# Token recurrence of a transformer kernel: one decay matrix and two products computed on GpSimd instead of VectorE

## The chip, the core and the metric

The kernel runs on one core of one Trainium2 chip. Its metric is the device time of one execution in microseconds (us), the median of three runs. In the rows PE is TensorE (PEld its weight loads), DVE is VectorE, ACT is ScalarE, POOL is GpSimd and SP is SyncE. All the matrices of this stage are float32 and lie in the on-chip memory SBUF, 128 partitions wide.

## The reference, cut to the stage that is changed

The reference is a decoder of twelve stages over 32 sequences of 64 tokens with 256 channels. The second stage is a recurrence over the tokens of each sequence, channel by channel. `k` is the layer-normed input, `v` the context, `w` and `u` are one number per channel:

```
def step(carry, kv_t):
    p, q, o = carry
    kt, vt = kv_t
    no = jnp.maximum(o, u + kt)
    A = jnp.exp(o - no)
    E = jnp.exp(u + kt - no)
    y = (A * p + E * vt) / (A * q + E)
    no2 = jnp.maximum(w + o, kt)
    A2 = jnp.exp(w + o - no2)
    E2 = jnp.exp(kt - no2)
    return ((A2 * p + E2 * vt, A2 * q + E2, no2), y)
...
x = x + _L0_xattn_ref(32, 64, 256, L0_xattn_w, L0_xattn_u, _layernorm(x, axis=-1), ctx_2048)
```

`E` is what the title calls the own factor: the weight of the token's own value `vt`.

## The kernel before, in words

The stages run one after the other, each in a block of its own that all engines enter and leave together. The changed stage is `l0_xattn`. It keeps channels on the 128 partitions and all 2048 tokens (32 sequences of 64) along a partition, so the 256 channels make two blocks, c = 0 and c = 1, and nearly every instruction covers 128 x 2048 elements.

VectorE carries the stage, in program order: `maxima(0)`, `maxima(1)`, `sums(0)`, `sums(1)`, `quotient(0)`, `quotient(1)`, `added(0)`, `added(1)`.

- `maxima(c)` fills `ws` (in the rows `wkv_ws`), the decay matrix: `w` of the channel in every column, and a very negative number in the first column of each of the 32 sequences, so that one scan can run over all sequences. It takes a memset to zero (L748), an addition of `w` (L751), and a small memset (L753). The scan L755 reads it and gives the running maxima `om`. From these come the exponents `a2`, `e2`, `e1`, `no`.
- `sums(c)` waits for ScalarE's exponentials, and runs the scans for `q` (`qb`, L771) and `p` (`pb`, L773). L775 and L777 make the denominator; L778 makes the prior part of the numerator, L779 the product of own factor `e1` (kept in `core_XN`) and value `v` (`core_CT`), L781 their sum.
- `quotient(c)` waits for ScalarE's reciprocal, `added(c)` adds the transposed result to the residual `X`.

ScalarE copies the shifted maxima (L809), takes the exponentials (L813 to L819; the semaphore `exp1_ready` rises after L819) and the reciprocals (L824, L826). TensorE transposes the context at the start and the results at the end. GpSimd has no instruction in this stage. The order on each engine is the order of the code; engines wait for each other by semaphores, and `drain()` makes an engine finish what it has begun before it goes on.

Of the kernel before, what the change touches and what calls it, by code (L numbers as in the profile page):

```python
# [17 lines left out]
ALU = mybir.AluOpType  # L18
# [3 lines left out]
P = 128  # L22
B, S, D = 32, 64, 256
TOK = B * S
NT = TOK // P
BPT = P // S
DC = D // P
# [677 lines left out]
NEG_INIT = -1e38  # L705


def l0_xattn(nc, g, a):

    with ExitStack() as ctx:  # L710
        s = Scope(nc, g, ctx, "wkv")
        wu = s.sb("wu", [P, 2, DC])
        tv, qb = s.sb("tv", [P, TOK]), s.sb("qb", [P, TOK + 1])
        loaded = s.sem("loaded")
# [5 lines left out]
        def early(sp):  # L720
# [6 lines left out]
        om, op, no, a2, e2 = [[s.sb(f"{n}{c}", [P, TOK]) for c in range(DC)] for n in ("om", "op", "no", "a2", "e2")]  # L727
        e1 = [xn[:, c, :] for c in range(DC)]
        ws = s.sb("ws", [P, TOK])
        pb = s.sb("pb", [P, TOK + 1])  # L730
        pt = s.ps("pt", [P, DC, NCH, CH])
        (ct_ready, ct_done, max_ready, prev_ready, decay_ready, own_ready, prior_ready, exp_ready, exp1_ready, den_ready, rcp_ready, yT_ready,
         t_ready) = s.sem(
            "ct_ready", "ct_done", "max_ready", "prev_ready", "decay_ready", "own_ready", "prior_ready", "exp_ready", "exp1_ready", "den_ready",
            "rcp_ready", "yT_ready", "t_ready")
        by_batch = lambda t: t[:, 0:TOK].rearrange("p (b t) -> p b t", t=S)
        with nc.Block() as block:

            @block.vector
            def _(dve):  # L740
                dve.memset(pb[:, 0:1], 0.0)
                dve.memset(qb[:, 0:1], 0.0)
                dve.wait_ge(loaded, 16)

                def maxima(c):
                    k = g.XT[:, c, :]
                    w, u = wu[:, 0, c:c + 1], wu[:, 1, c:c + 1]
                    dve.memset(ws[:, :], 0.0)  # L748
                    dve.memset(by_batch(op[c])[:, :, 0:1], NEG_INIT)
                    dve.drain()  # L750
                    dve.tensor_scalar(ws[:, :], ws[:, :], w, None, ALU.add)  # L751
                    dve.drain()
                    dve.memset(by_batch(ws)[:, :, 0:1], NEG_INIT)  # L753
                    dve.drain()
                    dve.tensor_tensor_scan(om[c][:, :], ws[:, :], k, NEG_INIT, ALU.add, ALU.max).then_inc(max_ready, 1)  # L755
                    dve.drain()
                    dve.tensor_tensor(e2[c][:, :], k, om[c][:, :], ALU.subtract)
                    dve.wait_ge(prev_ready, c + 1)
                    dve.scalar_tensor_tensor(no[c][:, :], k, u, op[c][:, :], ALU.add, ALU.max)
                    dve.scalar_tensor_tensor(a2[c][:, :], op[c][:, :], w, om[c][:, :], ALU.add, ALU.subtract).then_inc(decay_ready, 1)  # L760
                    dve.drain()
                    dve.scalar_tensor_tensor(e1[c], k, u, no[c][:, :], ALU.add, ALU.subtract).then_inc(own_ready, 1)
                    dve.tensor_tensor(no[c][:, :], op[c][:, :], no[c][:, :], ALU.subtract).then_inc(prior_ready, 1)

                def sums(c):
                    v = g.CT[:, c, :]
                    dve.wait_ge(exp_ready, c + 1)
                    if c == 0:
                        dve.wait_ge(ct_done, 1)
                    dve.tensor_tensor(tv[:, :], e2[c][:, :], v, ALU.mult)  # L770
                    dve.tensor_tensor_scan(qb[:, 1:TOK + 1], a2[c][:, :], e2[c][:, :], 0.0, ALU.mult, ALU.add)  # L771
                    dve.drain()
                    dve.tensor_tensor_scan(pb[:, 1:TOK + 1], a2[c][:, :], tv[:, :], 0.0, ALU.mult, ALU.add)  # L773
                    dve.wait_ge(exp1_ready, c + 1)
                    dve.tensor_tensor(om[c][:, :], no[c][:, :], qb[:, 0:TOK], ALU.mult)  # L775
                    dve.drain()
                    dve.tensor_tensor(om[c][:, :], om[c][:, :], e1[c], ALU.add).then_inc(den_ready, 1)  # L777
                    dve.tensor_tensor(op[c][:, :], no[c][:, :], pb[:, 0:TOK], ALU.mult)  # L778
                    dve.tensor_tensor(tv[:, :], e1[c], v, ALU.mult)  # L779
                    dve.drain()  # L780
                    dve.tensor_tensor(op[c][:, :], op[c][:, :], tv[:, :], ALU.add)  # L781
                    dve.drain()

                def quotient(c):
                    dve.wait_ge(rcp_ready, c + 1)
                    dve.tensor_tensor(op[c][:, :], op[c][:, :], om[c][:, :], ALU.mult).then_inc(yT_ready, 1)

                def added(c):
                    for n in range(NCH):
                        dve.wait_ge(t_ready, c * NCH + n + 1)  # L790
                        xs = g.X[:, n * TPC:(n + 1) * TPC, c * P:(c + 1) * P]
                        dve.tensor_tensor(xs, xs, pt[:, c, n, :].rearrange("p (j d) -> p j d", d=P), ALU.add)

                maxima(0)
                maxima(1)
                sums(0)
                sums(1)
                quotient(0)
                quotient(1)
                added(0)  # L800
                added(1)

            @block.scalar
            def _(act):
                act.preload_act_table_set("natural_log_exp_and_others")

                def previous(c):
                    act.wait_ge(max_ready, c + 1)
                    act.activation(by_batch(op[c])[:, :, 1:S], by_batch(om[c])[:, :, 0:S - 1], ACT.Copy).then_inc(prev_ready, 1)  # L809

                def exponentials(c):
                    act.wait_ge(decay_ready, c + 1)
                    act.activation(a2[c][:, :], a2[c][:, :], ACT.Exp)  # L813
                    act.activation(e2[c][:, :], e2[c][:, :], ACT.Exp)
                    act.drain().then_inc(exp_ready, 1)
                    act.wait_ge(own_ready, c + 1)
                    act.activation(e1[c], e1[c], ACT.Exp)
                    act.wait_ge(prior_ready, c + 1)
                    act.activation(no[c][:, :], no[c][:, :], ACT.Exp)  # L819
                    act.drain().then_inc(exp1_ready, 1)  # L820

                def reciprocals(c):
                    act.wait_ge(den_ready, c + 1)
                    act.activation(om[c][:, :], om[c][:, :], ACT.Ln)  # L824
                    act.drain()
                    act.activation(om[c][:, :], om[c][:, :], ACT.Exp, scale=-1.0).then_inc(rcp_ready, 1)  # L826

                def context():
                    for k in range(NCH * DC):
                        i, c = k // DC, k % DC  # L830
                        act.wait_ge(ct_ready, k + 1)
                        last = act.activation(g.CT[:, c, i * CH:(i + 1) * CH], pt[:, c, i, :], ACT.Copy)
                    last.then_inc(ct_done, 1)

                previous(0)
                context()
                exponentials(0)
                previous(1)
                exponentials(1)
                reciprocals(0)  # L840
                reciprocals(1)

            @block.tensor
            def _(pe):
                for i in range(NCH):
                    pe.wait_ge(cx_loaded[i], 16)
                    for c in range(DC):
                        for j in range(TPC):
                            mm = pe.transpose(pt[:, c, i, j * P:(j + 1) * P], cx[i][:, j, c * P:(c + 1) * P], g.ident[:, :])
                        mm.then_inc(ct_ready, 1)  # L850
                for c in range(DC):
                    pe.wait_ge(yT_ready, c + 1)
                    for n in range(NCH):
                        for j in range(TPC):
                            t0 = n * CH + j * P
                            mm = pe.transpose(pt[:, c, n, j * P:(j + 1) * P], op[c][:, t0:t0 + P], g.ident[:, :])
                        mm.then_inc(t_ready, 1)
# [2123 lines left out]


LEVELS = [l0_attn, l0_xattn, l0_ffn, l1_attn, l1_xattn, l1_ffn, l2_attn, l2_xattn, l2_ffn, l3_attn, l3_xattn, l3_ffn]


# [175 lines left out]
```

## Time and profile before

| | before |
|---|---|
| time, median of 3 runs | 4816.47 us (4814.08 to 4819.29) |
| time of the profiled execution | 4816.8 us |
| span of the profiled execution | 4815.0 us, mean granted TensorE clock 0.936 |
| the changed stage and its surroundings, 202 to 296 us | 94.0 us, 2.0% of the span |
| VectorE busy in those 94 us | 91.70 us |
| ScalarE / TensorE / GpSimd busy in them | 31.25 / 9.50 / 0.00 us |

The span runs from the first to the last instruction; 1.8 us of the time lie outside it. A row of the timeline gives start, duration, engine, line, operation, tile written and tiles read, shape, count and, in brackets, how long the engine had been idle and what ended that.

### The profile page before, as it was taken

The page shows a single profiled execution, that of the slowest core. Times are in us where ns is not written, and L with a number is a line of the kernel's source. Part 1 is how long each engine was busy: PE and PEld are TensorE (multiplying, and loading weights), DVE is VectorE, ACT ScalarE, POOL GpSimd, SP SyncE. Part 2 cuts the span into 40 slices and gives each one's busy share as a digit, 9 for nine tenths or more (in the row PEclk, how much of TensorE's full clock was granted, in tenths as well). Part 3 has the DMA queues.
Part 4 walks back from the last instruction along what each step waited for, and adds up shares of the span by engine and source line. Part 5 has one row for each costly group of instructions (what it writes and reads, how often), then busy time and mean ns, then how long its engine had stood idle before and what let it go on. Part 6 is the DMA issues. An engine that isn't in the chain of part 4 may idle for free. (4 is left out here: it accounts for less than half of the span.)

```text
span 4815.0 us, 142985 instructions
## 1 busy us (share of the span) xinstructions
PE 4134.3 (86%) x62044; PEld 2706.1 (56%) x62052; DVE 3237.9 (67%) x6019; ACT 2128.8 (44%) x3774; POOL 1514.5 (31%) x1605
## 2 busy tenths in 40 slices
PE   8527886677777887997999999999999999779999
PEld 6415654323325664443677777777777777445555
DVE  7897734788897787744677777777777777531111
ACT  3545533654444554322555555555555555221111
POOL 1001200198893220000344433443334433212222
PEclk9868987889889998998999999999999999789999
DMA  1000000133341001001000000000001000031111
GB/s 34 19 27 11 2 12 20 59 119 122 118 141 42 2 2 33 20 0 40 12 24 21 21 21 24 22 21 21 21 22 26 21 17 4 8 125 54 50 53 44
DMA packets 72967, 175.11 MB, mean 36 GB/s; under 512 B 14578, under 2 KB 27892, under 8 KB 69748
## 3 DMA queue, kind: packets, MB, share of 16 engines
q1 hardware_dynamic: 72340, 165.96, 11.1%
q8 instruction: 490, 8.03, 0.7%
q14 instruction: 137, 1.12, 0.1%
HBM read 163.04 MB, written 2.88 MB: 34 GB/s over the span
## 5 line engine op out<-in xcount | busy, mean ns | idle before, releaser
L1684 POOL TENSOR_TENSOR ssm_ub<-ssm_dtu,ssm_bcn 128x512 f32<-128x512 f32 x256 | 324.5, 1294 | 305.0 <-DMA ssm_bcn<-ssm_bct 302.6
L2437 POOL TENSOR_TENSOR dn_eb<-dn_ee,dn_cc 128x512 f32<-128x512 f32 x64 | 66.7, 1042 | 1043.4 <-DVE dn_cc L2551 1043.4
L2977 DVE TENSOR_TENSOR moe_hh<-moe_si,moe_pu 128x512 f32<-128x512 f32 x104 | 71.4, 687 | 450.6 <-PE moe_pu L2866 444.3
L2481 DVE SCALAR_TENSOR_TENSOR core_XN<-dn_bA,dn_w,core_XN 128x504 f32<-128x504 f32 (+2 forms) x384 | 280.6, 731 | 44.0 <-ACT core_XN L2318 24.0
L1583 ACT ACTIVATE ssm_da<-core_XN,ssm_al 128x504 f32<-128x504 f32 x240 | 163.2, 683 | 254.0 <-DVE ssm_ph L1751 169.4
L2144 PE MATMUL dn_bA<-core_XT,dn_w 128*128 128x512 f32 x512 | 259.3, 630 | 18.7 <-DVE core_XN L2481 13.4
L2910 ACT ACTIVATE moe_si<-moe_pg 128x512 f32<-128x512 f32 x104 | 62.1, 597 | 467.1 <-PE moe_pg L2866 467.1
L2929 POOL TENSOR_TENSOR moe_hw<-moe_hh,moe_cb 128x512 f32<-128x512 f32 x100 | 126.4, 1264 | 451.3 <-DVE moe_hh L2977 393.2
L1570 PE MATMUL ssm_py<-ssm_hc,core_ident 128*128 128x512 f32 x352 | 201.0, 674 | 65.0 <-DVE ssm_hc L1755 34.9
L2276 PE MATMUL dn_po<-dn_wo,dn_cT 128*128 128x256 f32 x1024 | 242.3, 390 | 3.3 <-issue 2.2
L1751 DVE TENSOR_TENSOR_SCAN ssm_ph<-ssm_da,ssm_ub 128x512 f32<-128x512 f32 x168 | 205.0, 1220 | 30.0 <-POOL ssm_ub L1684 17.1
L2168 PEld LDWEIGHTS dn_pm<-dn_XB,dn_mb 32*32 32x32 f32 x16384 | 166.8, 105 | 92.2 <-issue 86.4
L2419 POOL TENSOR_TENSOR dn_gm<-dn_cb,dn_cs 128x256 f32<-128x256 f32 x128 | 76.7, 620 | 447.6 <-DMA dn_cb<-dn_cum 447.6
L309 POOL TENSOR_TENSOR a_ke<-a_qkT,a_kmask 128x512 f32<-128x512 f32 (+1 forms) x96 | 85.5, 911 | 410.4 <-DVEq L600 303.8
L2168 PEld LDWEIGHTS dn_pm<-dn_zz,dn_XB 32*32 32x32 f32 x16384 | 164.8, 105 | 88.4 <-issue 87.7
L2276 PEld LDWEIGHTS dn_po<-dn_wo,dn_cT 128*128 128x128 f32 x1024 | 192.0, 192 | 31.1 <-issue 2.7
L2168 PE MATMUL dn_pm<-dn_XB,dn_mb 32*32 32x32 f32 x16384 | 195.8, 195 | 4.6 <-DVE dn_XB L2492 3.1
L2866 PE MATMUL moe_pg<-core_XT,moe_w 128*128 128x512 f32 x416 | 198.1, 599 | 0.0
L2866 PE MATMUL moe_pu<-core_XT,moe_w 128*128 128x512 f32 x416 | 195.5, 592 | 0.0
L2168 PE MATMUL dn_pm<-dn_zz,dn_XB 32*32 32x32 f32 x16384 | 193.2, 194 | 0.5 <-ACT dn_zz L2327 0.5
L2881 PE MATMUL moe_py<-moe_w,moe_hw 128*128 128x256 f32 x800 | 188.7, 379 | 0.0
L2881 PEld LDWEIGHTS moe_py<-moe_w,moe_hw 128*128 128x128 f32 x800 | 152.0, 190 | 62.4 <-issue 46.9
(521 smaller groups left out, 10450.2 us busy)
## 6 DMA issues: line engine op xcount, KB each, us to landing
ssm_bcn<-ssm_bct SPq DMA_DIRECT2D x128, 512.0 KB, 3.7
dn_cb<-dn_cum SPq DMA_DIRECT2D x32, 512.0 KB, 4.8
dn_w<-in_dn_w SPq DMA_DIRECT2D x32, 388.0 KB, 3.3
moe_cb<-moe_rows SPq DMA_DIRECT2D x64, 192.0 KB, 2.8
moe_w<-in_moe_w SPq DMA_DIRECT2D x26, 384.0 KB, 9.8
moe_cb<-moe_rows SPq DMA_DIRECT2D x64, 128.0 KB, 3.0
dn_wo<-in_dn_w SPq DMA_DIRECT2D x16, 256.0 KB, 5.1
moe_cb<-moe_rows SPq DMA_DIRECT2D x64, 64.0 KB, 2.6
```

The source lines that it names most:

```text
L309: last = pool.tensor_tensor(dst[:, c, :, :], bcm(src[:, c, :], R), bc(kmask[:, :], P), ALU.mult)
L1570: pe.matmul(py[:, turn_ % 2, :], g.ident[:, :], src[:, :], start=n == 0, stop=n == N - 1).then_inc(add_done, 1)
L1583: act.activation(nb(factor(u))[:, :, 1:S], nb(dt[q % 2][:, c, :])[:, :, 1:S], ACT.Exp, scale=al[:, n, c:c + 1]).then_inc(da_ready, 1)
L1684: pool.tensor_tensor(ub[u % NUB][:, :], dtu[q % 2][:, c, :], bcn[i % NB][:, 0, :], ALU.mult).then_inc(ub_ready, 1)
L1751: dve.tensor_tensor_scan(ph[:, m % 2, :], factor(u), ub[u % NUB][:, :], 0.0, ALU.mult, ALU.add).then_inc(scan_done, 1)
L2144: mm = pe.matmul(bank[:, :], wp[:, kc, gi * P:(gi + 1) * P], g.XT[:, kc, q * CH:(q + 1) * CH], start=kc == 0, stop=kc == DC - 1)
L2168: mm = pe.matmul(bank[r, n * HB:(n + 1) * HB], left(n, r), right(n, r), start=True, stop=True, tile_position=(q * HB, q * HB))
L2276: mm = pe.matmul(po[:, j // 2, (j % 2) * D:(j % 2 + 1) * D], cT[:, 2 * j + h, :], wo[o // NCH % 2][:, h, :], start=h == 0, stop=h == 1)
L2481: last = dve.scalar_tensor_tensor(dst[:, :, n:S], src[:, :, 0:S - n], w[i // NCH % 2][:, at:at + 1], dst[:, :, n:S], ALU.mult, ALU.add)
L2866: mm = pe.matmul(dst[:, m % 2, :], w[:, k, at:at + P], g.XT[:, kc, n * CH:(n + 1) * CH], start=kc == 0, stop=kc == DC - 1)
L2881: mm = pe.matmul(py[:, j, 0:D], h[:, j * P:(j + 1) * P], w[:, k, DC * 2 * P:], start=k == 0, stop=k == G - 1)
L2929: pool.tensor_tensor(hw[m % 3][:, :], hh[m % 3][:, :], cb[j % NCB][:, :], ALU.mult).then_inc(hw_ready, 1)
```

## The change

GpSimd gets instructions in this stage. It builds the second block's decay matrix in a tile of its own, `ws1`; VectorE still builds the first block's, and for c = 1 waits on `wait_ready` before the scan. GpSimd also computes the product of own factor and value for both blocks, into `ov0` and `ov1`, as soon as `exp1_ready` tells that the exponentials of the block are there; VectorE waits on `own_v_ready` where it adds the product. Two semaphores and three tiles of 128 x 2048 are new.

```diff
         by_batch = lambda t: t[:, 0:TOK].rearrange("p (b t) -> p b t", t=S)
+        ws1 = s.sb("ws1", [P, TOK])
+        ov = [s.sb(f"ov{c}", [P, TOK]) for c in range(DC)]
         with nc.Block() as block:
+
+            @block.gpsimd
+            def _(pool):
+                pool.wait_ge(loaded, 16)
+                pool.memset(ws1[:, :], 0.0)
+                pool.drain()
+                pool.tensor_scalar(ws1[:, :], ws1[:, :], wu[:, 0, 1:2], None, ALU.add)
+                pool.drain()
+                pool.memset(by_batch(ws1)[:, :, 0:1], NEG_INIT).then_inc(wait_ready, 1)
+                pool.wait_ge(ct_done, 1)
+                for c in range(DC):
+                    pool.wait_ge(exp1_ready, c + 1)
+                    pool.tensor_tensor(ov[c][:, :], e1[c], g.CT[:, c, :], ALU.mult).then_inc(own_v_ready, 1)
...
                 def maxima(c):
                     k = g.XT[:, c, :]
                     w, u = wu[:, 0, c:c + 1], wu[:, 1, c:c + 1]
-                    dve.memset(ws[:, :], 0.0)
                     dve.memset(by_batch(op[c])[:, :, 0:1], NEG_INIT)
-                    dve.drain()
-                    dve.tensor_scalar(ws[:, :], ws[:, :], w, None, ALU.add)
-                    dve.drain()
-                    dve.memset(by_batch(ws)[:, :, 0:1], NEG_INIT)
-                    dve.drain()
-                    dve.tensor_tensor_scan(om[c][:, :], ws[:, :], k, NEG_INIT, ALU.add, ALU.max).then_inc(max_ready, 1)
+                    if c == 0:
+                        dve.memset(ws[:, :], 0.0)
+                        dve.drain()
+                        dve.tensor_scalar(ws[:, :], ws[:, :], w, None, ALU.add)
+                        dve.drain()
+                        dve.memset(by_batch(ws)[:, :, 0:1], NEG_INIT)
+                        dve.drain()
+                    else:
+                        dve.wait_ge(wait_ready, 1)
+                    dve.tensor_tensor_scan(om[c][:, :], (ws, ws1)[c][:, :], k, NEG_INIT, ALU.add, ALU.max).then_inc(max_ready, 1)
...
                     dve.tensor_tensor(op[c][:, :], no[c][:, :], pb[:, 0:TOK], ALU.mult)
-                    dve.tensor_tensor(tv[:, :], e1[c], v, ALU.mult)
                     dve.drain()
-                    dve.tensor_tensor(op[c][:, :], op[c][:, :], tv[:, :], ALU.add)
+                    dve.wait_ge(own_v_ready, c + 1)
+                    dve.tensor_tensor(op[c][:, :], op[c][:, :], ov[c][:, :], ALU.add)
```

On VectorE, in the second `maxima`, the row behind the last row of `maxima(0)` and up to the first of the exponents stood before as follows (the scans are printed as SCALAR_TENSOR_TENSOR).

```order
L763 TENSOR_TENSOR wkv_no<-wkv_op,wkv_no 128x2048
L748 MEMSET wkv_ws 128x2048
L749 MEMSET wkv_op 128x32
L751 TENSOR_SCALAR wkv_ws<-wkv_ws,wkv_wu 128x2048
L753 MEMSET wkv_ws 128x32
L755 SCALAR_TENSOR_TENSOR wkv_om<-wkv_ws,core_XT 128x2048
L757 TENSOR_TENSOR wkv_e<-core_XT,wkv_om 128x2048
```

And now, at the same place:

```order
L781 TENSOR_TENSOR wkv_no<-wkv_op,wkv_no 128x2048
L763 MEMSET wkv_op 128x32
L773 SCALAR_TENSOR_TENSOR wkv_om<-wkv_ws,core_XT 128x2048
L775 TENSOR_TENSOR wkv_e<-core_XT,wkv_om 128x2048
L777 SCALAR_TENSOR_TENSOR wkv_no<-core_XT,wkv_wu,wkv_op 128x2048
```

Three rows on the decay matrix are gone from there; in each `sums` the row of L779 is gone likewise. On GpSimd, between the stage of attention before it (a_xs, a_ke) and the next one, this now stands (before, nothing stood between the branch of L290 and that of L292).

```order
L290 UNCONDITIONAL_BRANCH
L741 UNCONDITIONAL_BRANCH
L744 MEMSET wkv_ws 128x2048
L746 ISA
L746 TENSOR_SCALAR wkv_ws<-wkv_ws,wkv_wu 128x2048
L748 MEMSET wkv_ws 128x32
L752 TENSOR_TENSOR wkv_ov<-core_XN,core_CT 128x2048 x2
L739 UNCONDITIONAL_BRANCH
L292 UNCONDITIONAL_BRANCH
```

The five operations have come to GpSimd; here `wkv_ws` stands for the new tile `ws1`, since the rows leave numbers out.

## Rows read from the trace of the kernel before

**Rows 1.** Page head.
```profile
span 4815.0 us, 142985 instructions
```

**Rows 2.** Windows, one stretch: length, PE, PEld, DVE, ACT, POOL busy; clock.
```profile
202.00:296.00 94.00, 9.50 (x64) 9.02 (x63) 91.70 (x46) 31.25 (x23) 0.00 (x0) 0.55 0.00 0
```

**Rows 3.** Waits from 201 to 310 us, row on the memsets: total, times, longest.
```profile
DVE wkv_ws L748 <- issue: 0.8, 2, 0.4
```

**Rows 4.** Timeline of VectorE in the stage.
```profile
204.28 1.28 DVE L751 TENSOR_SCALAR wkv_ws<-wkv_ws,wkv_wu 128x2048 f32<-128x2048 f32 x1
...
205.85 4.42 DVE L755 TENSOR_TENSOR_SCAN wkv_om<-wkv_ws,core_XT 128x2048 f32<-128x2048 f32 x1
...
219.55 2.28 DVE L763 TENSOR_TENSOR wkv_no<-wkv_op,wkv_no 128x2048 f32<-128x2048 f32 x1
222.21 1.76 DVE L748 MEMSET wkv_ws<- 128x2048 f32 x1 [0.38 <-issue]
...
225.69 4.42 DVE L755 TENSOR_TENSOR_SCAN wkv_om<-wkv_ws,core_XT 128x2048 f32<-128x2048 f32 x1
...
257.17 2.28 DVE L778 TENSOR_TENSOR wkv_op<-wkv_no,wkv_pb 128x2048 f32<-128x2048 f32 x1
...
259.37 2.28 DVE L779 TENSOR_TENSOR wkv_tv<-core_XN,core_CT 128x2048 f32<-128x2048 f32 x1
261.72 2.29 DVE L781 TENSOR_TENSOR wkv_op<-wkv_op,wkv_tv 128x2048 f32<-128x2048 f32 x1
...
286.60 4.49 DVE L786 TENSOR_TENSOR wkv_op<-wkv_op,wkv_om 128x2048 f32<-128x2048 f32 x2
```

**Rows 5.** Timeline of ScalarE in the stage.
```profile
222.85 1.89 ACT L819 ACTIVATE wkv_no<-wkv_no 128x2048 f32<-128x2048 f32 x1
...
242.68 1.89 ACT L819 ACTIVATE wkv_no<-wkv_no 128x2048 f32<-128x2048 f32 x1
...
281.78 1.91 ACT L826 ACTIVATE wkv_om<-wkv_om 128x2048 f32<-128x2048 f32 x1
```

**Rows 6.** Groups of GpSimd's instructions by shape: busy, mean ns, idle before.
```profile
L2434 POOL TENSOR_SCALAR dn_wo<-dn_wo,dn_nw 128x512 f32<-128x512 f32 x16 | 25.1, 1567 | 0.0
...
L2699 POOL TENSOR_TENSOR core_XN<-core_XN,lk_gb 128x1024 f32<-128x1024 f32 x4 | 9.4, 2348 | 42.2 <-ACT core_XN L2674 42.2
...
L296 POOL MEMSET a_ve<- 128x1024 f32 x3 | 2.8, 952 | 270.6 <-SPq L290 248.1 <-POOLq L111 22.5
```

**Rows 7.** L1751's instructions by source: min/median/max ns; `ssm_da` in PSUM, `ssm_dx` in SBUF.
```profile
L1751 DVE TENSOR_TENSOR_SCAN ssm_ph<-ssm_da,ssm_ub x168: 1203/1222/1232, 937.3 to 1470.2; 128x512 f32<-128x512 f32 x168
L1751 DVE TENSOR_TENSOR_SCAN ssm_ph<-ssm_dx,ssm_ub x8: 1204/1714/2223, 981.6 to 1395.8; 128x512 f32<-128x512 f32 x8
```

**Rows 8.** Timeline of VectorE and GpSimd around 981 us.
```profile
981.60 1.21 DVE L1751 TENSOR_TENSOR_SCAN ssm_ph<-ssm_dx,ssm_ub 128x512 f32<-128x512 f32 x1
981.76 2.10 POOL L1673 TENSOR_TENSOR ssm_hp<-ssm_hb,ssm_bcn 128x512 f32<-128x512 f32 x1 [3.24 <-DVE ssm_hb L1746]
```

**Rows 9.** The same from 4167 to 4175 us; all tiles in SBUF.
```profile
4167.04 1.40 DVE L2723 TENSOR_TENSOR_SCAN lk_st<-lk_kd,lk_xi 128x512 f32<-128x512 f32 x1 [1.71 <-ACT lk_xi L2662]
4167.31 3.28 POOL L2695 TENSOR_TENSOR core_X<-core_X,lk_gb 128x1024 f32<-128x1024 f32 x1
4169.55 2.13 DVE L2723 TENSOR_TENSOR_SCAN lk_st<-lk_kd,lk_xi 128x512 f32<-128x512 f32 x1 [0.33 <-ACT lk_xi L2662]
4170.55 3.26 POOL L2695 TENSOR_TENSOR core_X<-core_X,lk_gb 128x1024 f32<-128x1024 f32 x1
4172.52 1.57 DVE L2730 TENSOR_SCALAR lk_mr<-lk_ms 128x512 f32<-128x512 f32 x1
4174.02 0.41 DVE L2730 TENSOR_SCALAR lk_mr<-lk_ms 128x512 f32<-128x512 f32 x1
```

**Rows 10.** The same around 445 us; all tiles in SBUF.
```profile
445.22 2.14 DVE L628 TENSOR_TENSOR a_sc<-a_sc,a_mx 128x512 f32<-128x512 f32 x2
445.34 1.47 POOL L309 TENSOR_TENSOR a_ke<-a_qkT,a_kmask 128x512 f32<-128x512 f32 x1 [1.13 <-ACTq L498]
```

More of the change, by code:

```diff
@@ L732, in l0_xattn @@
         (ct_ready, ct_done, max_ready, prev_ready, decay_ready, own_ready, prior_ready, exp_ready, exp1_ready, den_ready, rcp_ready, yT_ready,
-         t_ready) = s.sem(
+         t_ready, wait_ready, own_v_ready) = s.sem(
             "ct_ready", "ct_done", "max_ready", "prev_ready", "decay_ready", "own_ready", "prior_ready", "exp_ready", "exp1_ready", "den_ready",
-            "rcp_ready", "yT_ready", "t_ready")
+            "rcp_ready", "yT_ready", "t_ready", "wait_ready", "own_v_ready")
         by_batch = lambda t: t[:, 0:TOK].rearrange("p (b t) -> p b t", t=S)
+        ws1 = s.sb("ws1", [P, TOK])
+        ov = [s.sb(f"ov{c}", [P, TOK]) for c in range(DC)]
         with nc.Block() as block:
+            @block.gpsimd
[10 more added lines that the diff above has]
+                    pool.tensor_tensor(ov[c][:, :], e1[c], g.CT[:, c, :], ALU.mult).then_inc(own_v_ready, 1)
             @block.vector
```

## The prediction

> **What bounds the kernel now.** I read the table of windows first. The changed stage is 94 us of a span of 4815 us, and VectorE is busy in 91.7 of them, with ScalarE at a third and GpSimd at nothing [rows 1, 2]. So VectorE alone sets the length of this stage. The table of waits confirms it: VectorE waits for no other engine there, and the only entry is 0.4 us of "issue" ahead of each of the two long memsets [rows 3]. The timeline of VectorE then gives the prices: the instructions stand back to back, a product of 128x2048 every 2.20 us where no drain lies between, and a scan takes 4.42 us [rows 4]. Whatever VectorE loses or gains here, the stage loses or gains, since the block ends with VectorE's additions, and the next stage cannot begin before. Last I looked for places elsewhere in the trace at which GpSimd and VectorE work on SBUF at the same time, because the stage has none of its own. They decide the case.
>
> **What VectorE is relieved of.** The second `maxima`: L763 ends at 219.55 + 2.28 = 221.83, and the scan L755 starts at 225.69 [rows 4]. In these 3.86 us stand the two memsets, the addition and three drains. One small memset (0.09) stays, so 3.8 us go. The gap of 0.38 us ahead of the long memset goes with it; it belongs to that memset. The products: L779 starts 2.20 us behind L778, and L781 follows as before, behind a drain [rows 4]. Removed in both `sums`: 4.4 us. Together VectorE has **8.2 us** less of its own work. Nothing takes its place as a dependence: the second `maxima` and the last steps wait for ScalarE as little as before. The tightest is the last reciprocal, ready at 281.78 + 1.91 = 283.69 [rows 5]. `quotient(1)`, the second of the pair from 286.60, started at about 288.8 [rows 4]; counted from the denominator that the reciprocal waits for, it now comes the 2.2 us of one product earlier, at 286.6, and 2.9 us remain.
>
> **Whether GpSimd is in time.** Its product for c = 0 can start when `exp1_ready` rises, at 222.85 + 1.89 = 224.74, and VectorE wants it behind L778, at 259.45; for c = 1 it is 244.57 [rows 4, 5] against about 282. The decay matrix is wanted at 221.8. GpSimd needs a few us for each, so the two new waits cost nothing, and neither does the later end of GpSimd in the block. The price lies elsewhere.
>
> **What GpSimd's instructions do to VectorE.** Of the scans L1751, the 168 that read their factor from PSUM took 1203 to 1232 ns; the 8 that read both inputs from SBUF took 1204 to 2223 ns [rows 7]. The timeline shows why. At 4167.04 a scan with both inputs in SBUF runs till 4168.44. GpSimd's L2695, begun at 4167.31, ends at 4170.59, 2.15 us behind the scan's end, although this shape takes 2.35 alone. The next scan begins at 4169.55 and ends at 4171.68, 1.09 behind GpSimd's end (alone 1.21 [rows 8]). GpSimd's next ends at 4173.81, 2.13 behind that scan, and L2730, an addition on VectorE that takes 0.41 alone, ends 0.28 behind that, after 1.57 [rows 6, 9]. They take turns: one runs, the other stands still. Around 981 us it is the same at 512 elements: GpSimd ends 1.05 behind the scan [rows 8]. And VectorE having the next instruction ready does not keep GpSimd out: the two L628 back to back took 2.14 us where two of that length take 1.3 (2.28 / 4 plus some start each), with GpSimd's instruction ending 0.55 us ahead of the pair's end [rows 4, 10]. All work of VectorE in this stage from L751 on has two SBUF inputs, or is the addition L751 that behaves as L2730. So each of GpSimd's three long instructions stops VectorE for about its own length, and VectorE has no idle time to take it from.
>
> Prices. The product: GpSimd ended 1.05 us behind the scan at 512 elements and 2.14 at 1024, so 1.09 per 512 more, and 2.14 + 2 x 1.09 = 4.3 at 2048 (alone 2.35 + 2 x 1.09 = 4.5). VectorE gets back some 0.1 of it, because the waiting instruction has already started up. That gives 4.2 us per product, **8.4** for two. The product for c = 0 falls behind the second L755, the one for c = 1 behind the first L771; each arrives while a scan runs and goes before the next instruction.
>
> The addition on GpSimd: there is only one size of it, 1567 ns at 512 [rows 6]. With the 0.2 us that does not scale (2.35 less two times 1.09) it is 0.2 + 4 x 1.37 = 5.7 us at 2048; by plain scaling it would be 6.3. GpSimd's memset of 1024 took 0.95 [rows 6], so 1.9 here; from the block's start near 201.9 the addition begins at about 203.9, before VectorE reaches its own, 204.28 [rows 4]. VectorE's then ends at 209.6 + 1.15 = 210.8 instead of 205.56: 5.2 us. If VectorE comes first, GpSimd waits till 205.56 and holds up the scan of 205.85 until 211.1: 5.2 again. So the order there does not matter, and I take **5.2**. The memset on GpSimd I cost at nothing: it reads nothing, and no row has one beside such work; if it holds up VectorE's memset too, 1.9 us are to be added. The small memset on GpSimd and the two more semaphores to be cleared lie beside VectorE's work.
>
> The sum: 4816.8 - 8.2 + 8.4 + 5.2 = **4822.2 us** against the profiled execution's own time. That execution lies 0.3 above the median, so the median should be 4821.9; I give 4822. Bounds: with nothing lost, 4808.6; with plain scaling of both (4.7 per product, 6.3 for the addition), -8.2 + 9.4 + 6.3 = +7.5, 4824.3.
>
> The rows show the losses at 0.2 to 0.4 us below GpSimd's own lengths. The Trainium skill, SBUF — State Buffer, section "SBUF: two separate sides", has the rule: VectorE and GpSimd share one pair of ports by an exclusive lock that is held for a whole instruction, against VectorE's instructions with two SBUF inputs (when GpSimd's reads SBUF) or in a two-port mode. By the whole instruction the losses would be 4.5, 4.5 and 5.7, and the time 4823.3. This rule speaks against the change, the trace agrees with it up to those tenths, and I go by the rows.
>
> **The rivals.**
> - *Only the products stop VectorE.* No row has GpSimd's addition beside a scan; it reads one tile, and might be let through. Then 4816.8 - 8.2 + 8.4 = 4817.0. Against it speaks that VectorE's own one-tile addition L2730 took its turn too. Chance 12%.
> - *The offload is hidden, as it looks in the code.* GpSimd beside VectorE for nothing: 4808.6. Rows 7 to 10 speak against it; for it only that the 168 scans with one input in PSUM were untouched, and no such scan is in this stage. 6%.
> - *Slower by more than 0.2%, because GpSimd works slower on these shapes.* There is no row of 2048 elements on GpSimd. At the addition's price per element (1567 ns for 512) a product would take 6.3 too: 3 x 6.3 - 8.2 = +10.7, 4827.5. It decides from 17.8 us of lost time on, where I count 13.6. The product rows at 512 and 1024 agree on 2.1 ns per element, which speaks against it. 7%.
>
> **How the numbers follow.** The forecast, three turns lost and 8.2 us gained, has 70%, with 4820 to 4824.5 as its own range. 5% are left for things that I did not think of. 0.2% of the time is 9.6 us, about what a measurement of this kernel can tell from no change (its three runs lie 5.2 us apart). The forecast is +0.11%, the first rival 0.0%, the second -0.17%: all within it. So the chances are 3% faster (the second rival with luck), 88% same, 9% slower (the third, and part of the unforeseen). The range for 8 times in 10 takes in the forecast, most of the first rival and the upper bounds: 4815.5 to 4826.
>
> **What the changed profile would show.** VectorE's group of L767 (the addition for c = 0) or the first L773 takes some 5 us more than 1.28 or 4.42. Two more of its instructions take some 4.2 us longer than their like: the one behind the second L773, and the one behind the first L789. GpSimd's two L752 take more than 4.5 us, since they wait for a scan's end. VectorE shows no wait for GpSimd. The stage, 94 us before, is some 99 us long. I would be wrong if these durations stand at 1.28, 2.29 and 4.42, or if VectorE waits for `wait_ready` or `own_v_ready`.

## The result, and the profile after

Twelve runs of the changed kernel have a median of 4831.2 us (4824.0 to 4837.0), and those of the kernel before one of 4822.2. One of these twelve took 11938 us and is not in the ratio; the median of the other eleven is 4821.1. The ratio is 1.0018, with a 95% interval of 1.0010 to 1.0027: slower by some 9 us, where 5.4 was forecast. The interval does not contain 1. The 4831.2 lies above the predicted range, whose upper end was 4826 and which had been built on the first three runs of before (median 4816.5). The profiled execution took 4831.6 us.

The table of windows from the first instruction of the stage's block on VectorE to the first of the next stage: length, then PE, PEld, DVE, ACT and POOL busy, granted clock, DMA. Before:

```profile
201.88:296.29 94.41, 9.62 (x64) 9.14 (x64) 91.79 (x48) 31.40 (x24) 0.00 (x0) 0.55 0.00 0
```

The changed kernel:

```profile
207.05:305.99 98.94, 8.87 (x64) 8.39 (x64) 97.04 (x43) 31.40 (x24) 21.62 (x5) 0.55 0.00 0
```

The block is 4.5 us longer, with five instructions fewer on VectorE. The timeline of VectorE in the changed kernel shows where; the lines answer to [rows 4], and ... marks lines left out:

```profile
207.58 1.76 DVE L765 MEMSET wkv_ws<- 128x2048 f32 x1 [0.35 <-issue]
209.43 6.13 DVE L767 TENSOR_SCALAR wkv_ws<-wkv_ws,wkv_wu 128x2048 f32<-128x2048 f32 x1
...
215.85 4.42 DVE L773 TENSOR_TENSOR_SCAN wkv_om<-wkv_ws,core_XT 128x2048 f32<-128x2048 f32 x1
...
229.55 2.28 DVE L781 TENSOR_TENSOR wkv_no<-wkv_op,wkv_no 128x2048 f32<-128x2048 f32 x1
231.79 4.39 DVE L773 TENSOR_TENSOR_SCAN wkv_om<-wkv_ws,core_XT 128x2048 f32<-128x2048 f32 x1
...
236.27 6.36 DVE L775 TENSOR_TENSOR wkv_e<-core_XT,wkv_om 128x2048 f32<-128x2048 f32 x1
...
253.92 4.42 DVE L789 TENSOR_TENSOR_SCAN wkv_qb<-wkv_a,wkv_e 128x2048 f32<-128x2048 f32 x1
258.41 8.50 DVE L791 TENSOR_TENSOR_SCAN wkv_pb<-wkv_a,wkv_tv 128x2048 f32<-128x2048 f32 x1
...
271.37 2.28 DVE L796 TENSOR_TENSOR wkv_op<-wkv_no,wkv_pb 128x2048 f32<-128x2048 f32 x1
273.73 2.29 DVE L799 TENSOR_TENSOR wkv_op<-wkv_op,wkv_ov 128x2048 f32<-128x2048 f32 x1
```

And that of GpSimd, which had nothing there before:

```profile
206.98 1.81 POOL L744 MEMSET wkv_ws<- 128x2048 f32 x1 [27.75 <-SPq L739]
209.04 5.45 POOL L746 TENSOR_SCALAR wkv_ws<-wkv_ws,wkv_wu 128x2048 f32<-128x2048 f32 x1 [0.25 <-issue]
214.60 1.05 POOL L748 MEMSET wkv_ws<- 128x32 f32 x1
234.92 5.56 POOL L752 TENSOR_TENSOR wkv_ov<-core_XN,core_CT 128x2048 f32<-128x2048 f32 x1 [19.26 <-ACTq L838]
254.81 7.82 POOL L752 TENSOR_TENSOR wkv_ov<-core_XN,core_CT 128x2048 f32<-128x2048 f32 x1 [14.33 <-ACTq L838]
```

Read the two side by side. GpSimd's addition runs from 209.04 to 214.49. VectorE's own, L767, is on record from 209.43 and ends at 215.56, 1.07 us behind GpSimd's; it takes 6.13 us instead of 1.28. GpSimd's first product is on record from 234.92, but the scan ends at 236.18 and the product at 240.48, 4.3 behind it; L775, next on VectorE, ends 2.15 behind that and takes 6.36 us instead of 2.29. The second product ends at 262.63, 4.3 behind the scan L789, and L791 takes 8.50 instead of 4.42. So these long instructions hold a wait inside their recorded durations. VectorE counts as busy in it, and no entry of its table of waits (what waited for what: us in total, times, longest) names GpSimd:

```profile
DVE wkv_ws L765 <- issue: 0.4, 1, 0.4
DVE wkv_pb L756 <- PEq L111: 0.3, 1, 0.3
DVE ln0f_st L127 <- PEq L739: 0.3, 1, 0.3
```

### The profile page after: what moved, and what is told of

It reads as the page before. It is cut to its first block and busy times, and to the rows that moved or that the text cites. A ratio compares the mean times of both kernels' runs of the same rounds, so it can differ in the third digit from the quotient of the medians.

```text
span 4829.8 us, 142995 instructions
## 1 busy us (share of the span) xinstructions
PE 4142.3 (86%) x62052; PEld 2717.0 (56%) x62052; DVE 3243.1 (67%) x6014; ACT 2129.3 (44%) x3774; POOL 1536.3 (32%) x1610
```

## The experiments

Stage lengths below are those of the block as in the two window rows: 94.4 us before. Ratios are to the runs of before that were taken together with that experiment, with 95% intervals; experiments of one group (e1 to e4, e5 to e8, e9 to e12, e13 to e15) share these runs. Each experiment has one trace.

### The same kernels again: e1, e2, e12, e15

No edit. Expected of e1 and e15 (before):

> The kernel before, unchanged, traced a second time. In the trace of the changed kernel the stage of the recurrence is 5.4 us longer than before (from the first normalization behind it back to the one ahead of it: 114.0 us instead of 108.6), but 4.2 us of the 14.8 us by which its span is longer lie ahead of the stage, where the two kernels have the same instructions, and 5.2 us behind it. Theory A: those 9.4 us are the scatter between executions. Then this second trace shows the stage within 0.3 us of the first, and the parts ahead of and behind it off by several us in all. Theory B: the parts outside the stage repeat to within 1 us, and the changed kernel lengthens them. Then this trace matches the first one everywhere within about 1 us. Ratio to before: 1.000.

> The kernel before against itself once more on the same chip as the two padded ones: 1.000 if a kernel that is loaded anew has no offset of its own. 1.0004 was measured the first time.

Expected of e2 and e12 (changed):

> The changed kernel traced a second time. Theory A (scatter outside the stage): the stage is again 5.4 us longer than before within 0.3 us; the parts ahead of and behind it are off by several us, not by the same amounts as in the first trace; ratio near 1.001. Theory B (the change itself lengthens other parts): ahead of the stage +4.2 us and behind it +5.2 us again, ratio near 1.003.

> The changed kernel beside the three others on the same chip. The block of the stage is 98.9 us again. Scatter: a ratio anywhere from 1.0008 to 1.0018, whose mean with the first two (1.0018, 1.0017) comes nearer to 1.001. A true extra loss outside the block: 1.0017 again.

In the table, "ahead" runs from VectorE's first normalization to that of the changed stage, "state space" is the stage of [rows 7] with its normalization, "delta rule" the longest stage; all from the timelines, in us. e10 is told further down.

| | ahead | block | state space | delta rule | span | ratio |
|---|---|---|---|---|---|---|
| before | 182.4 | 94.4 | 590.8 | 1923.9 | 4815.0 | |
| e1, before | 184.9 | 94.4 | 594.8 | 1920.6 | 4814.4 | 1.0004 (0.9995 to 1.0013) |
| e15, before | 182.4 | 94.5 | 593.6 | 1923.6 | 4814.8 | 0.9991 (0.9981 to 1.0000) |
| after | 186.6 | 98.9 | 596.2 | 1923.5 | 4829.8 | 1.0018 (1.0010 to 1.0027) |
| e2, after | 182.6 | 98.9 | 597.2 | 1920.8 | 4826.6 | 1.0017 (1.0008 to 1.0026) |
| e12, after | 188.9 | 99.5 | 597.5 | 1924.2 | 4834.8 | 1.0021 (1.0012 to 1.0030) |
| e10, padded | 182.4 | 99.1 | 593.6 | 1927.0 | 4826.5 | 1.0021 (1.0013 to 1.0030) |

The block repeats to 0.1 us, but for the third trace of the changed kernel, where the last additions waited for TensorE's transposes. Everything else moves by several us between executions of one kernel, and a kernel compared with itself came out at 1.0004 once and at 0.9991 once. For e1 theory A (scatter) held: the block repeated to 0.03 us, the stretch ahead moved by 2.5 and the two long stages by 4 and 3. For e2 neither held whole: the parts moved as A has it, but the ratio lies between those of the two theories (1.001 and 1.003). e12's 1.0021 lies above what its expectation allowed to scatter (1.0018).

This movement goes with TensorE's clock. The 116 runs of before in the four groups have these means by the granted clock of the whole run (1 is full speed):

| granted clock | 0.932 | 0.933 | 0.934 | 0.935 | 0.936 | 0.937 | 0.938 |
|---|---|---|---|---|---|---|---|
| runs | 2 | 4 | 22 | 41 | 35 | 9 | 3 |
| mean time, us | 4834.2 | 4829.8 | 4826.7 | 4823.0 | 4819.6 | 4816.7 | 4812.6 |

That is some 3.5 us for each thousandth. The stretch ahead of the changed stage shows the same: it took 182.4 to 182.6 us in the traces in which it was granted 0.99 (before, e2, e10, e15), 184.9 at 0.98 (e1), 186.6 at 0.96 (after) and 188.9 at 0.95 (e12). The clock does not account for the changed kernel's excess, though: its own runs have means of 4832.1 at 0.934 (7 runs) and 4830.7 at 0.935 (12), 5 and 8 us above those of before at the same clock.

Here is one place where the level changes, instruction by instruction: the eight transposes of each quarter of the normalization ahead of the block, in the timeline of before, and then of the changed kernel:

```profile
195.66 1.94 PE L199 MATMUL ln0x_pt<-core_ident,core_XN 128*128 128x128 f32 x8 [0.19 <-ACT core_XN L171]
197.80 1.17 PE L199 MATMUL ln0x_pt<-core_ident,core_XN 128*128 128x128 f32 x8 [0.20 <-ACT core_XN L171]
199.75 1.07 PE L199 MATMUL ln0x_pt<-core_ident,core_XN 128*128 128x128 f32 x8 [0.78 <-ACT core_XN L171]
```

```profile
199.96 1.94 PE L199 MATMUL ln0x_pt<-core_ident,core_XN 128*128 128x128 f32 x8 [0.20 <-ACT core_XN L171]
202.09 3.90 PE L199 MATMUL ln0x_pt<-core_ident,core_XN 128*128 128x128 f32 x16 [0.20 <-ACT core_XN L171]
```

The same instructions take 1.07 us at the clock of 2.4 GHz and 1.94 at 1.2; before was granted the higher one after two quarters, the changed kernel in this execution was not (mean granted clock of the stretch 0.64 and 0.54 of full speed). The normalization took 14.2 us or 15.1 accordingly, and both values occur with either kind of kernel: 14.2 in before, e1, e15 and in e12, 15.1 in after, e2 and in e9 to e11. It stands in none of the columns of the table.

### One part alone: e3 (decay matrix), e4 (products)

e3 leaves the products on VectorE and keeps GpSimd's decay matrix; e4 the reverse. Of each edit one pair of lines is shown; the memsets, drains and waits that belong to them move along:

```diff
 # e3
-                    pool.tensor_tensor(ov[c][:, :], e1[c], g.CT[:, c, :], ALU.mult).then_inc(own_v_ready, 1)
+                    dve.tensor_tensor(tv[:, :], e1[c], v, ALU.mult)
 # e4
-                pool.tensor_scalar(ws1[:, :], ws1[:, :], wu[:, 0, 1:2], None, ALU.add)
+                    dve.tensor_scalar(ws[:, :], ws[:, :], w, None, ALU.add)   (for both blocks)
```

> Only the second block's decay matrix is on GpSimd; the products stay on VectorE. By the theory of turns: VectorE's addition for the first block takes 6.1 us instead of 1.28, which costs 4.9, and the second block saves 3.8 to 3.9, so the stage is about 1.0 us longer than before. By the rival that GpSimd's addition is let through: the stage is 3.8 us shorter. If the slow small memset on GpSimd (1.05 us) mattered, the scan would wait too; it should not.

> Only the two products are on GpSimd; both decay matrices are built on VectorE. By the theory of turns: each product stops VectorE for about 4.1 us and saves 2.2, so the stage is about 3.8 us longer than before. By the rival that the two engines only share some bandwidth, the instruction beside GpSimd's would be spread out by less and the stage about as long as before or 4.4 us shorter if nothing is lost.

Measured: e3 95.2 us, 0.8 longer than before (ratio 1.0013, 1.0004 to 1.0022); e4 97.8, 3.4 longer (1.0007, 0.9998 to 1.0016). Together 4.2 of the 4.5. In e3 VectorE's addition for the first block is long again, with no product on GpSimd:

```profile
206.80 6.13 DVE L763 TENSOR_SCALAR wkv_ws<-wkv_ws,wkv_wu 128x2048 f32<-128x2048 f32 x1
```

So the rival that the addition is let through beside VectorE falls: it was to shorten the block by 3.8. In e4 the first product came before the scan and not behind it; the timelines of VectorE and of GpSimd:

```profile
227.10 0.09 DVE L762 MEMSET wkv_ws<- 128x32 f32 x1
227.26 8.34 DVE L764 TENSOR_TENSOR_SCAN wkv_om<-wkv_ws,core_XT 128x2048 f32<-128x2048 f32 x1
```

```profile
226.51 4.81 POOL L746 TENSOR_TENSOR wkv_ov<-core_XN,core_CT 128x2048 f32<-128x2048 f32 x1 [51.42 <-ACTq L829]
```

Here GpSimd's product goes first: VectorE's addition had ended at 226.97, GpSimd's product ends at 231.32, 4.35 behind it, and the scan pays 3.9 us. The small memset in between, which reads nothing, keeps its 0.09 us.

### Each product twice: e5

```diff
+                    pool.tensor_tensor(ov[c][:, :], e1[c], g.CT[:, c, :], ALU.mult)
+                    pool.drain()
                     pool.tensor_tensor(ov[c][:, :], e1[c], g.CT[:, c, :], ALU.mult).then_inc(own_v_ready, 1)
```

> The changed kernel with each product computed twice on GpSimd (same tile, same values). VectorE's own work is unchanged. By the theory of turns each extra product stops VectorE once more for its own length less some tenths: two more of VectorE's instructions are 4.1 us longer, and the stage is 8.2 to 8.4 us longer than that of the changed kernel, 13.7 us longer than before. If VectorE could go on beside GpSimd once it had waited, or if GpSimd's instruction were kept out by a back-to-back queue of VectorE, the stage would stay as it is.

Measured: 107.6 us, 8.7 longer than the changed kernel, ratio 1.0041 (1.0029 to 1.0053). The timeline of VectorE shows that its next instruction standing ready does not keep GpSimd out: beside the addition, four instructions are long now.

```profile
233.72 6.36 DVE L777 TENSOR_TENSOR wkv_e<-core_XT,wkv_om 128x2048 f32<-128x2048 f32 x1
240.00 6.58 DVE L779 SCALAR_TENSOR_TENSOR wkv_no<-core_XT,wkv_wu,wkv_op 128x2048 f32<-128x2048 f32 x1
...
260.10 8.50 DVE L793 TENSOR_TENSOR_SCAN wkv_pb<-wkv_a,wkv_tv 128x2048 f32<-128x2048 f32 x1
268.52 6.51 DVE L795 TENSOR_TENSOR wkv_om<-wkv_no,wkv_qb 128x2048 f32<-128x2048 f32 x1
```

The second of a pair costs 4.23 and 4.25 us, a tenth or two more than the first. In both pairs no drain of VectorE lies between the two; that this is the reason was not tested.

### The decay matrices on ScalarE: e6

The products are on VectorE as before, GpSimd has nothing, and both matrices come from ScalarE:

```diff
+                def decay(c):
+                    act.activation((ws, ws1)[c][:, :], g.XT[:, c, :], ACT.Identity, bias=wu[:, 0, c:c + 1], scale=0.0)
+                    act.drain()
+                    act.activation(by_batch((ws, ws1)[c])[:, :, 0:1], by_batch((ws, ws1)[c])[:, :, 0:1], ACT.Copy,
+                                   scale=0.0, bias=NEG_INIT).then_inc(wait_ready, 1)
...
+                act.wait_ge(loaded, 16)
+                decay(0)
+                decay(1)
                 previous(0)
```

> Both decay matrices are built by ScalarE (activation with the channel's w as bias), which waits for 7.2 us at the start of the stage; the products stay on VectorE, GpSimd has nothing. ScalarE does not take turns with VectorE by the theory, since they run side by side throughout the stage. VectorE loses 3.8 us of its work in the second block, and in the first it waits for ScalarE (table load till 203.1, then 1.9 and about 0.3) instead of its own 4 us, which gains some 0.5. The stage is about 4.3 us shorter than before; ratio 0.999. If any engine beside VectorE cost it time, the stage would be about as long as before.

Measured: 90.1 us, 4.3 shorter than before, as expected; the ratio, 1.0002 (0.9993 to 1.0010), does not show it. ScalarE fills the second matrix while VectorE's first scan, with two inputs in SBUF, takes its usual 4.42 us:

```profile
208.80 1.99 ACT L805 ACTIVATE wkv_ws<-core_XT,wkv_wu 128x2048 f32<-128x2048 f32 x1
```

```profile
208.93 4.42 DVE L752 TENSOR_TENSOR_SCAN wkv_om<-wkv_ws,core_XT 128x2048 f32<-128x2048 f32 x1 [3.42 <-ACT wkv_ws L807]
```

So a matrix made beside VectorE does not stop it when the engine is ScalarE. Only the first one is waited for (3.42 us): the first scan starts 3.6 us behind the block's first instruction, where it was 4.0 before.

### One input in PSUM: e7 and e8

Both are e4 with each product held back until VectorE begins the two scans of its own block (`tv_ready`). In e8 ScalarE also writes the exponential that both scans read to PSUM:

```diff
 # e7 and e8
+                    pool.wait_ge(tv_ready, c + 1)
 # e8
+        ax = [pt[:, c, :, :].rearrange("p n t -> p (n t)") for c in range(DC)]
-                    act.activation(a2[c][:, :], a2[c][:, :], ACT.Exp)
+                    act.wait_ge(ct_done, 1)
+                    act.activation(ax[c], a2[c][:, :], ACT.Exp)
-                    dve.tensor_tensor_scan(qb[:, 1:TOK + 1], a2[c][:, :], e2[c][:, :], 0.0, ALU.mult, ALU.add)
+                    dve.tensor_tensor_scan(qb[:, 1:TOK + 1], ax[c], e2[c][:, :], 0.0, ALU.mult, ALU.add)
```

> As the kernel with only the products on GpSimd, but each product waits until VectorE begins the two scans of its own block, which read both inputs from SBUF. By the theory of turns this changes the place and not the price: each product stops one scan for 4.1 us or more, and the stage is some 3.8 us longer than before, as without the delay. It is the partner of the next run.

> The same, but ScalarE writes the exponential of the decay (one input of both scans) to PSUM, so that the scans beside GpSimd's products have only one input in SBUF. By the theory of turns through SBUF's second way in, nothing is lost: the scans take 4.4 us each, GpSimd's products 4.5, and the stage is 4.4 us shorter than before (perhaps a few tenths less for reads of PSUM). By the rival that GpSimd stops VectorE whatever it reads, the stage is 3.8 us longer than before, as in the run with the scans in SBUF.

Measured: e7 98.0 us (3.6 longer than before; 1.0009, 1.0000 to 1.0017), e8 90.1 us (4.35 shorter; 0.9990, 0.9980 to 1.0000). The scans of the first block and GpSimd's product beside them, in the timelines of e7:

```profile
244.46 4.42 DVE L781 TENSOR_TENSOR_SCAN wkv_qb<-wkv_a,wkv_e 128x2048 f32<-128x2048 f32 x1
248.95 8.49 DVE L783 TENSOR_TENSOR_SCAN wkv_pb<-wkv_a,wkv_tv 128x2048 f32<-128x2048 f32 x1
```

```profile
244.72 8.44 POOL L747 TENSOR_TENSOR wkv_ov<-core_XN,core_CT 128x2048 f32<-128x2048 f32 x1 [69.95 <-DVE wkv_tv L780]
```

And in those of e8:

```profile
246.13 4.42 DVE L782 TENSOR_TENSOR_SCAN wkv_qb<-wkv_pt,wkv_e 128x2048 f32<-128x2048 f32 x1
250.62 4.43 DVE L784 TENSOR_TENSOR_SCAN wkv_pb<-wkv_pt,wkv_tv 128x2048 f32<-128x2048 f32 x1
```

```profile
246.39 4.49 POOL L748 TENSOR_TENSOR wkv_ov<-core_XN,core_CT 128x2048 f32<-128x2048 f32 x1 [69.93 <-DVE wkv_tv L781]
```

The same two engines, the same work at the same place: with two inputs in SBUF they take turns (GpSimd 8.44, the second scan 8.49), with one in PSUM neither notices the other (4.49 for GpSimd, 4.42 and 4.43 for the scans, and the same in the second block). For the products this tells the cause. For the addition it does not: VectorE's addition reads one tile in SBUF and is stopped all the same (6.13 instead of 1.28 us), and no run varies where that one reads from.

### Both gains together: e9

e8 with e6's decay matrices.

> The version that the experiments point to: both decay matrices on ScalarE, both products on GpSimd beside scans that read one input from PSUM. The two gains were measured apart, as 4.3 us and 4.35 us of the stage's block (from its first instruction on VectorE to the first of the next stage: 94.4 us before). If they add up, the block is 85.7 to 85.9 us long and the time 8.7 us shorter, ratio 0.998. If they get in each other's way (ScalarE now has the decay matrices and a reading wait more), it is nearer to 90.

Measured: block 86.2 us, 8.2 shorter than before; ratio 0.9979 (0.9970 to 0.9988), median 4811.7 us against 4821.7 for before. It beats both kernels. Some 0.3 us of the expected gain is missing. It goes at the end, where the last additions wait for transposes at the low clock, 0.16 us of it on record in one place:

```profile
285.44 3.19 DVE L798 TENSOR_TENSOR core_X<-core_X,wkv_pt 128x512 f32<-128x512 f32 x5
288.80 2.12 DVE L798 TENSOR_TENSOR core_X<-core_X,wkv_pt 128x512 f32<-128x512 f32 x3 [0.16 <-PE wkv_pt L872]
```

### A delay with nothing on GpSimd: e10, e11, e13, e14

The kernel before, with n needless products (2.3 to 2.4 us each with its drain) in the second block:

```diff
+                    for _ in range(n * c):
+                        dve.tensor_tensor(ws[:, :], k, k, ALU.mult)
+                        dve.drain()
                     dve.memset(ws[:, :], 0.0)
```

> The kernel before with two needless products of 128x2048 and their drains on VectorE ahead of the second block's decay matrix, so that its block is 4.6 us longer than before, as the changed kernel's is 4.5; GpSimd has nothing there. The output is that of before. The open question: the changed kernel's runs are 8 us longer in the median, its block only 4.5. Theory S (scatter and the place of the run in time): the rest has nothing to do with GpSimd; either a mere delay of 4.6 us costs 8 us too (ratio 1.0017), or the rest is scatter and the ratio is 1.0010. Theory G (GpSimd's work or the new tiles lengthen something else): this kernel's ratio is 1.0010 and the changed kernel's stays 1.0017.

> The same with six products and drains: the block is 13.8 us longer than before, about as in the kernel that computes each product twice on GpSimd (13.2), whose runs were 19.8 us longer in the median. If a mere delay gives the rest too, the ratio is 1.004; if the time grows by the block alone, it is 1.0029.

> The kernel before with one needless product and drain on VectorE in the second block: its block is 2.3 to 2.4 us longer. If a delay costs its own length and the rest is scatter, the ratio is 1.0005. If any delay, or any change to the program, costs some 4 us more (as 4.6 us of delay did, with 1.0021), the ratio is 1.0013.

> The same with three: the block is 7.0 us longer. Length alone gives 1.0015; some 4 us more give 1.0023.

| n | block, longer than before | ratio (interval) | in us |
|---|---|---|---|
| 1 | 2.5 | 1.0006 (0.9997 to 1.0015) | 3 |
| 2 | 4.6 | 1.0021 (1.0013 to 1.0030) | 10 |
| 3 | 7.0 | 1.0011 (1.0002 to 1.0020) | 5 |
| 6 | 14.1 | 1.0035 (1.0022 to 1.0047) | 17 |

Two products give the changed kernel's ratio with nothing on GpSimd, three give less than two. A constant extra of 4 us for any delay was to give 1.0013 for n = 1 and 1.0023 for n = 3: the second lies outside its interval, the first inside, so n = 3 alone speaks against it. Over the sixteen comparisons of this study the time's difference (from the ratio) less the block's lies between -4 and +7 us, with a mean of 2 and a standard deviation of 3; an unchanged kernel against itself gave +2 and -4.

## Why the prediction was right or wrong

- **What bounds the stage**: right. VectorE had no slack, and the block's length followed its work and its stops in every run, in e6 and e9 with a wait of 3.42 us for ScalarE's first matrix.
- **That GpSimd's instructions stop VectorE one for one**: right. For the products (e4, e5) the reason given, two inputs in SBUF, is shown by e7 against e8. For the addition the stop is shown (e3) and its reason is not: it reads one tile, and the prediction took it from its like, L2730. The prediction's "all work of VectorE in this stage from L751 on has two SBUF inputs" overlooks the last eight additions (L792), which read `wkv_pt` in PSUM; it did not matter, since GpSimd had long ended. The three instructions named were the ones that grew. The first rival (the addition is let through) and the second (hidden) fell, and so did the third: GpSimd's product takes 4.49 us undisturbed (e8), where 4.5 had been worked out from 1024 elements, and not 6.3.
- **The terms**: each loss too large by little. The products cost 4.07 and 4.08 (4.2 each was taken), the addition 4.85 (5.2), for the most part because GpSimd's took 5.45 and not 5.7. VectorE was relieved of 8.3 (8.2): L781 ends at 231.83 and the scan starts at 231.79, which is 3.9, and twice 2.2. The final additions were 0.1 shorter. The terms add up to +4.6 and the block measured +4.5, where +5.4 was forecast. The memset on GpSimd did cost VectorE's memset nothing (1.76 in both).
- **The time**: wrong, and by two steps that had nothing to do with the mechanism. The first is the level that the sum starts from, 4816.8, less 0.3 for the median. It took three runs within 5.2 us of each other for the level of the kernel. The eleven that count in the result give 4821.1, 4.6 higher, and the 27 to 33 runs of each later group 4821.5 to 4823.4. The second is that the sum has no term for the time outside the block: it was put at nothing, and no reason was given. The measured difference is 8 to 10 us (three times: 1.0018, 1.0017, 1.0021) and the block's 4.5. One of the four padded kernels had as much (e10, 10 us for a block 4.6 longer) with nothing on GpSimd; the scatter of the comparisons, 3 us, covers one such result, and less well three of them. In the traces of the changed kernel the state-space stage took 596 to 597.5 us and in those of before 591 to 595, but e6 and e7, without GpSimd's decay matrix, had 600 and 597.5, and e13, with nothing on GpSimd, 597.6, so I can't tie that to the change. Whether some 3 to 5 us outside the block belong to it stays open. The range was too narrow for either step: its upper end left 4 us above the forecast, and the level alone moved by some 5. The sign is the forecast one, and the ratio stayed within the 0.2% to which 88% had been given.

## What to carry to other kernels

Before moving work from VectorE to GpSimd, look at where the neighbours on VectorE read from: beside instructions with two inputs in SBUF, a product that takes GpSimd twice as long as VectorE stops VectorE for 4.1 us to save it 2.2, and the profile books it as VectorE being busy. One-input work can be stopped as well: the addition was, for 4.85 us, while memsets were not. The same move paid in full when the scans beside it read one input from PSUM (4.35 us of the 4.4), and so did work that went to ScalarE. And where an effect is a thousandth of the time, predict and measure the stage's block in the trace; for the total, ask first how far more runs would move the reference.

## What the runs showed of the hardware

- GpSimd's memset of 32 single elements, 64 apart, on 128 partitions took 1.05 us (L748), VectorE's of the same shape 0.09. It cost nothing here.
- GpSimd's addition of a column's number took 5.45 us at 2048 elements and 1.57 at 512 [rows 6]: 2.53 ns for each element more.
- A scan on VectorE reads PSUM as fast as SBUF: 4.42 us at 128x2048 from either (e8, e7).
- TensorE's granted clock changed level at different points of the same instruction sequence from one execution to another, and moved a normalization by 0.9 us. Over 116 runs of one kernel, a thousandth less of the granted clock went with some 3.5 us more of the time.
